# A two-layer gated recurrence and FFN kernel: a new order of all engines, more dummy transposes, h in two buffers

## The reference, cut to what matters

```python
tf    = sigmoid(sum(cond, -1))
decay = exp(-exp(w)) * (0.5 + 0.5 * tf)                 # per batch and channel
ek    = exp(min(F, 30));  ekv = ek * F
nf, df = scan forward of (ekv, ek);  nb, db = scan backward    # a = a * decay + in
euk   = exp(min(u + F, 30))
num   = nf + nb - ekv + euk * F;  den = df + db - ek + euk
y     = sigmoid(x) * num / max(den, 1e-8) * (0.8 + 0.2 * tf)
# layer 0: x += (expert e = argmax(softmax(y @ Wg.T)); prob * 4 * (y @ A[e].T) @ B[e].T)
# layer 1: x += gelu(y @ q(w1).T + b1) @ q(w2).T + b2     # q: sign where |w| >= 0.7 * mean|w|
```

## Time and profile before

| what | value |
|---|---|
| median of 3 runs | 109.0 us (108.44 to 109.6) |
| profiled execution: its time | 109.72 us |
| its span in the profile | 107.9 us |
| TensorE busy | 96.6 us, 90% |
| VectorE busy | 90.7 us, 84% |
| ScalarE busy | 80.4 us, 75% |
| GpSimd busy | 66.3 us, 61% |

### The profile page before, as it was taken

The page is one execution under the profiler, slowest core; times in us unless marked ns, Lnnn a source line. Parts: engine busy times, 40 slices in busy tenths (PEclk is TensorE's granted clock), DMA queues, the critical chain, the costliest instruction groups (busy, mean ns, idle before and its releaser), DMA issues. The chain is left out here.

```text
span 107.9 us, 2103 instructions
## 1 busy us (share of the span) xinstructions
PE 96.6 (90%) x650; PEld 86.6 (80%) x650; DVE 90.7 (84%) x204; ACT 80.4 (75%) x144; POOL 66.3 (61%) x87
## 2 busy tenths in 40 slices
PE   4989958479999989999999998999998897899990
PEld 2759748468789879987988978989998796799980
DVE  3389999959939999999999999799999988968320
ACT  4377998999718689499896599877986699475520
POOL 4179999499920581665998869995755554031220
PEclk9999999965599999999999999999999999999999
DMA  1889999200000000000000000000000001300005
GB/s 61 224 289 319 265 295 399 108 3 0 0 0 0 3 0 6 0 0 0 0 0 3 6 0 0 0 0 0 0 0 6 0 0 54 140 6 3 0 0 194
DMA packets 6886, 6.43 MB, mean 60 GB/s; under 512 B 2370, under 2 KB 6492, under 8 KB 6876
## 3 DMA queue, kind: packets, MB, share of 16 engines
q1 hardware_dynamic: 6868, 6.31, 18.5%
q10 hardware_dynamic: 8, 0.00, 0.0%
HBM read 5.26 MB, written 1.05 MB: 58 GB/s over the span
## 5 line engine op out<-in xcount | busy, mean ns | idle before, releaser
L789 DVE TENSOR_TENSOR_SCAN run<-bank,kv 128x256 f32<-128x256 f32 x32 | 20.3, 671 | 0.2
L300 POOL TENSOR_TENSOR h_lo<-h,h_hi 128x512 fp32r<-128x512 f32 x7 | 9.8, 1409 | 13.3 <-DVE h_hi L308 8.3
L1220 PE MATMUL bank<-xin_hi,w1T 128*128 128x256 f32 x64 | 16.3, 292 | 1.6 <-DVE xin_lo L294 0.9
L1152 PE MATMUL bank<-num,AT 128*128 128x256 f32 x64 | 17.5, 424 | 0.1
L1254 PE MATMUL bank<-w2T,h_hi 128*128 128x256 f32 x64 | 15.9, 285 | 0.3 <-DVE h_lo L300 0.3
L606 ACT ACTIVATE h<-bank,bT 128x256 f32<-128x256 f32 x32 | 13.2, 483 | 3.7 <-DVE h_lo L300 3.0
L1254 PE MATMUL bank<-w2T,h_lo 128*128 128x256 f32 x64 | 15.6, 282 | 0.0
L1220 PE MATMUL bank<-xin_lo,w1T 128*128 128x256 f32 x64 | 15.5, 279 | 0.0
L1152 PEld LDWEIGHTS bank<-num,AT 128*128 128x128 f32 x64 | 13.1, 214 | 2.2 <-issue 0.2
L1168 PE MATMUL bank<-hm,BT 128*128 128x256 f32 x64 | 14.6, 381 | 0.0
L248 POOL TENSOR_TENSOR num<-num,own 128x512 f32<-128x512 f32 x7 | 9.2, 1319 | 8.4 <-DVE num L823 8.4
(11 more groups left out here) (140 smaller groups left out, 232.6 us busy)
## 6 DMA issues: line engine op xcount, KB each, us to landing
w_nat<-in_L_ffn_w_dram SPq DMA_DIRECT2D x2, 1024.0 KB, 8.5
F_nat<-in_fside_BxSxS_dram SPq DMA_DIRECT2D x4, 256.0 KB, 3.5
x_nat<-in_x_dram SPq DMA_DIRECT2D x4, 256.0 KB, 4.9
out_dram<-outb SPq DMA_DIRECT2D x3, 256.0 KB, 2.1
A_nat<-in_L_ffn_A_dram SPq DMA_DIRECT2D x1, 512.0 KB, 5.8
B_nat<-in_L_ffn_Bw_dram SPq DMA_DIRECT2D x2, 256.0 KB, 6.5
out_dram<-outb SPq DMA_DIRECT2D x2, 128.0 KB, 1.9
wv_rows<-in_L_cond_w_dram SPq DMA_DIRECT2D x2, 1.0 KB
```

Of the source, the lines that this page charges most:

```text
L300: eng.tensor_tensor(h_lo[:, b % 2, 2 * j:2 * j + 2], h32[:, 2 * j:2 * j + 2], h_hi[:, b % 2, 2 * j:2 * j + 2].bitcast(F32), ALU.subtract). ...
L789: dve.tensor_tensor_scan(run[:, r, c, q], decay_ps[:, l, c, b:b + 1].broadcast_to([P, T]), kv[:, b, c, q], 0.0, ALU.mult, ALU.add).then_in ...
L1152: mm = pe.matmul(bank[H_BANK + k][:, (m % 2) * T:(m % 2 + 1) * T], AT[:, c, m * P:(m + 1) * P], num_at(0, b)[:, c], start=(c == 0), stop=( ...
L1220: mm = pe.matmul(bank[g_bank[g]][:, (f % 2) * T:(f % 2 + 1) * T], w1T[:, c, f * P:(f + 1) * P], part[:, b % 2, c], start=(c == 0 and part ...
```

## The change

h32 gets a second buffer, chosen by b % 2; the gelu then waits for h_low of b - 2, and h_high waits for h_low of b - 1. For layer 1's gate, the 1 is added to tanh on GpSimd for all four batches, by a function of its own with two scalar operations (multiply by 1, add 1), and `times_tanh` is a plain multiply on either engine. `warm_up(3)` becomes `warm_up(4)`, and of `keep_warm` 8, 18 and 6 become 0, 19 and 27. All four written orders change.

```diff
-        h32 = sb("h32", [P, NF, T])
+        h32 = sb("h32", [P, 2, NF, T])
...
+        def add_one(b):
+
+            nc.gpsimd.wait_ge(tanh_ready, b + 1)
+            nc.gpsimd.tensor_scalar(sig[:, b], sig[:, b], 1.0, 1.0, ALU.mult, ALU.add).then_inc(one_added, 1)
+
         def times_tanh(eng, b):
-
             r, u = ring(1, b)
-            eng.wait_ge(tanh_ready, b + 1)
-            if eng is nc.vector:
-                eng.wait_ge(num_ready[r], u + 1)
-                eng.scalar_tensor_tensor(num_at(1, b), sig[:, b], 1.0, num_at(1, b), ALU.add, ALU.mult).then_inc(nsig_ready[b], 1)
-            else:
-                eng.tensor_scalar(sig[:, b], sig[:, b], 1.0, None, ALU.add).then_inc(one_added[b], 1)
-                eng.wait_ge(one_added[b], 1)
-                eng.wait_ge(num_ready[r], u + 1)
-                eng.tensor_tensor(num_at(1, b), num_at(1, b), sig[:, b], ALU.mult).then_inc(nsig_ready[b], 1)
+            eng.wait_ge(one_added, b + 1)
+            eng.wait_ge(num_ready[r], u + 1)
+            eng.tensor_tensor(num_at(1, b), num_at(1, b), sig[:, b], ALU.mult).then_inc(nsig_ready[b], 1)
...
         def h_high(eng, b, j):
             eng.wait_ge(h32_ready, NF * b + 2 * j + 2)
+            if b:
+                eng.wait_ge(hlo_ready[j], b)
...
             def gelus(b, j):
                 act.wait_ge(g_psum, NJ * b + j + 1)
-                if b:
-                    act.wait_ge(hlo_ready[j], b)
+                if b >= 2:
+                    act.wait_ge(hlo_ready[j], b - 1)
...
             hidden(3, 0)
             hidden(3, 1)
-            ffn_out(2, 0, 0)
-            ffn_out(2, 0, 1)
-            hidden(3, 2)
             ffn_out(2, 1, 0)
             ffn_out(2, 1, 1)
+            hidden(3, 2)
```

More of the change, by code:

```diff
@@ L420, in _ @@
             gains()
-            clip_keys(pool, 1)
+            times_values(pool, 0)
             factors()
-            times_values(pool, 0)
+            seed(pool, 0, 0, DEN)
+            seed(pool, 0, 1, DEN)
+            seed(pool, 0, 0, NUM)
             times_values(pool, 1)
@@ L426, in _ @@
             clip_keys(pool, 2)
-            seed(pool, 0, 0, NUM)
-            seed(pool, 0, 1, DEN)
-            own_values(pool, 0, 1)
-            times_values(pool, 2)
             add_num(pool, 0, 0)
             times_sigmoid(pool, 0)
+            own_values(pool, 0, 1)
             seed(pool, 0, 1, NUM)
@@ L676, in _ @@
             gelus(0, 0)
+            copy_mask(3)
             gelus(0, 1)
-            copy_mask(3)
+            h_high(act, 0, 0)
+            gelus(0, 2)
+            gelus(0, 3)
+            h_high(act, 0, 1)
             tanh(2)
-            gelus(0, 2)
-            h_high(act, 0, 0)
+            h_high(act, 0, 3)
             h_high(act, 0, 2)
-            h_high(act, 0, 1)
-            gelus(0, 3)
-            xin_high(act, 1)
             act.preload_act_table_set("natural_log_exp_and_others")
             log_den(1, 2)
-            h_high(act, 0, 3)
             reciprocal(1, 2)
@@ L703, in _ @@
             reciprocal(1, 3)
+            result(act, 1)
             act.preload_act_table_set("gelu_and_others")
-            gelus(2, 0)
-            result(act, 0)
             gelus(2, 1)
-            result(act, 1)
+            h_high(act, 2, 1)
             gelus(2, 2)
@@ L909, in _ @@
             forward_chunk(0, 0, DEN, 1)
+            clip_keys(dve, 1)
             inverse_gains()
-            seed(dve, 0, 0, DEN)
             forward(0, 1, DEN)
+            forward(0, 0, NUM)
             place_factors()
@@ L953, in _ @@
-            gate(2)
-            backward(0, 3, DEN)
-            own_keys(1, 0)
-            add_den(0, 3)
-            gate_index(2)
+            forward(0, 2, NUM)
+            forward(0, 3, DEN)
+            select_expert(0, 1)
+            gate(1)
+            select_expert(0, 0)
+            add_den(0, 2)
+            backward(0, 2, NUM)
+            gate_index(1)
+            forward(0, 3, NUM)
+            expert_mask(1)
+            own_keys(1, 0)
+            den_times_rec(0, 2)
+            backward(0, 3, DEN)
@@ L958, in _ @@
+            ratio(0, 2)
+            select_expert(1, 1)
+            select_expert(1, 0)
+            add_den(0, 3)
+            forward(1, 0, NUM)
+            gate(2)
+            backward(0, 3, NUM)
+            gate_index(2)
+            forward(1, 0, DEN)
+            den_times_rec(0, 3)
+            expert_mask(2)
             backward(1, 0, NUM)
             backward(1, 0, DEN)
-            den_times_rec(0, 3)
+            ratio(0, 3)
+            select_expert(2, 0)
             add_den(1, 0)
-            expert_mask(2)
@@ L992, in _ @@
-            add_num(dve, 1, 2)
-            h_low(dve, 0, 3)
-            times_tanh(dve, 2)
-            refine_rec(1, 2)
-            seed(dve, 1, 3, DEN)
-            product(1, 2)
-            h_high(dve, 1, 2)
+            select_expert(3, 0)
+            select_expert(3, 1)
+            refine_rec(1, 1)
+            forward(1, 2, DEN)
+            product(1, 1)
+            xin_high(dve, 1)
+            backward(1, 2, DEN)
+            add_den(1, 2)
+            forward(1, 2, NUM)
+            forward(1, 3, DEN)
@@ L999, in _ @@
+            backward(1, 2, NUM)
+            den_times_rec(1, 2)
+            forward(1, 3, NUM)
+            times_tanh(dve, 2)
+            seed(dve, 1, 3, NUM)
+            seed(dve, 1, 3, DEN)
+            refine_rec(1, 2)
+            product(1, 2)
+            h_low(dve, 0, 3)
             h_low(dve, 1, 1)
@@ L1001, in _ @@
             backward(1, 3, DEN)
+            backward(1, 3, NUM)
             add_den(1, 3)
-            backward(1, 3, NUM)
-            h_low(dve, 1, 3)
+            add_num(dve, 1, 3)
+            h_high(dve, 2, 0)
+            times_tanh(dve, 3)
             den_times_rec(1, 3)
-            times_tanh(dve, 3)
             refine_rec(1, 3)
@@ L1343, in _ @@
             ffn_out(1, 2, 1)
-            hidden(2, 2)
+            place_output(2)
             ffn_out(1, 3, 0)
             ffn_out(1, 3, 1)
+            hidden(2, 2)
             hidden(2, 3)
-            place_output(2)
+            ffn_out(2, 0, 0)
+            ffn_out(2, 0, 1)
             place_output(3)
```

241 lines of the change are left out of this document (109 added, 132 removed).

## The result

The changed kernel took 102.95 us (median of 4 runs, 102.38 to 104.0) against 108.72 for the kernel before on the same chip (4 runs, 108.12 to 109.6): a ratio of 0.942, 95% interval 0.935 to 0.950. Two later comparisons on other chips gave 0.940 (0.934 to 0.947) and 0.943 (0.938 to 0.949). The forecast was 105.3 us with a range of 103.9 to 108.0: right in sign, with a gain too small by 2.3 us, and outside its range. The profiled execution took 102.58 us, its span is 100.8.

What follows compares the result with a forecast made beforehand. It took TensorE and VectorE as nearly level bounds. TensorE's -1.0 (start), -1.96 (clock) and 0.7 of idle gave -3.7, span 107.9 to 104.2, or 105.3 us against the median; range 103.9 to 108.0.

Steps and rivals of the forecast that it cites:

- Both are bounds, nearly level ... TensorE is late first: From 31.43 to 93.35 TensorE idles 2.98 us; VectorE is busy 65.81 of 71.18; a gain in one alone is not kept.
- 2.98 us of idle of which the order can take some. I count 0.7 as taken. That gives -3.7 for TensorE: TensorE behind the first mask: 0.7 us of its idle time removed, on top of -2.96 at the mask, gives -3.7.
- The last xin_lo could end at 86.8 without waits: VectorE from the first ratio at 21.6: 64.2 us of work plus 1.0 of small gaps, against 93.29 before.
- I count about 3 (three locks of 1, a stall of 0.5): VectorE's waits up to the last xin_lo, about 3 us on top of 86.8, where 3.8 were allowed.
- Start of the expert products, "-1.0": TensorE's expert products wait for ScalarE's whole BT copy, expected at 23.65: start at 23.85 instead of 24.84.
- Clock, 1.96 us: More dummy transposes keep TensorE at 2.4 GHz through the first expert products: gain 1.96 us, bounds 0 to 1.96 + 0.84.
- First ratio "to about 21.6": VectorE up to the first ratio: -0.44 us from moved own keys and clip_keys(1), from 22.11 to about 21.6 with the seed.
- Tail, -1.0: ffn_out(2, 0) ahead of hidden(3, 0): 88 matmuls instead of 96 follow the last xin_lo, 10.6 us for 11.59.
- A: TensorE's clock falls all the same near the first expert products, costing 1.96 us back: 107.3 us; chance 0.18.
- B: VectorE keeps the pace: waits for GpSimd's num and seeds use 2 us more than counted: 107.2 us; chance 0.14.
- C: GpSimd falls behind between own_values(1, 1) and add_num(1, 2), VectorE's tanh waits: slower, 110.3 if 5 us late; chance 0.05.
- D: No change: first ratio slips from 21.6 to 23 behind GpSimd's clip_keys(2), TensorE loses the clock: 108.7 us; chance 0.08.

Runs made afterwards that it cites:

- before, new dummies: Kernel before with 19, 29 and 10 dummy transposes in place of 8, 18 and 6, nothing else changed: 0.989 of the kernel before.
- before, TensorE +1.78: Kernel before with TensorE's residual products of batch 2 issued three times, 1.78 us more work: 1.002 of the kernel before.
- before, VectorE +2.36: Kernel before with four more scans to a spare buffer on VectorE, 2.36 us more work: 1.028 of the kernel before.
- before, nine steps moved: Kernel before with nine VectorE steps of batch 2 in another order, such as the multiply by tanh ahead of h_lo(0,3): 0.990 of the kernel before.
- early part alone: Kernel before with the new order only up to the first ratio and first expert products, with 19 and 27 dummies: 0.988 of the kernel before.
- early part, nine steps moved: Kernel before with the new order up to the first expert products, plus nine VectorE steps of batch 2 reordered: 0.978 of the kernel before.
- late part alone: Changed kernel with the old order and old dummies up to the first ratio and first expert products: 0.969 of the kernel before.
- changed, old tail: Changed kernel with ffn_out(2, 0) behind hidden(3, 1) again: 0.952 of the kernel before, median 104.8 us.
- changed, TensorE +1.78: Changed kernel with TensorE's residual products of batch 2 issued three times, 1.78 us more work: 0.950 of the kernel before.
- changed, VectorE +2.36: Changed kernel with four more scans to a spare buffer on VectorE, 2.36 us more work: 0.962 of the kernel before.
- section 1: Extra work on TensorE or VectorE alone: 1.002 and 1.028 in the kernel before, 0.950 and 0.962 in the changed kernel, all against the kernel before.
- section 4: Nine VectorE steps of batch 2 reordered: 0.990 in the kernel before, 0.978 in it with the new order up to the first expert products.
- section 6: Changed kernel repeated: 0.940 and 0.943; with four more dummies 0.942; with ScalarE's cast xin_hi(2) ahead of gelus(1, 3) 0.947, all against the kernel before.
- section 3: Changed kernel with the old 8, 18, 6 dummies: 0.947; kernel before with 19, 29, 10: 0.989, both against the kernel before.
- section 5: Changed kernel with add_one in its old form 0.951, on VectorE for batches 2 and 3 0.954, one h buffer 0.950, ffn_out(2, 0) moved back 0.952.
- the run with the slow add_one: Changed kernel with the four GpSimd add_one in the old form, one scalar operation, 1.50 us for 0.62: 0.951 of the kernel before.

## Why the forecast was wrong in size

The table holds the profiled executions: start of the second ratio and of the last xin_lo on VectorE, the time between, the span, and what lies behind the last xin_lo.

| kernel | second ratio | last xin_lo | between | span | behind |
|---|---|---|---|---|---|
| before | 29.30 | 92.60 | 63.3 | 107.9 | 15.3 |
| before, new dummies | 28.85 | 92.03 | 63.2 | 107.3 | 15.3 |
| before, TensorE +1.78 | 29.42 | 92.30 | 62.9 | 107.6 | 15.3 |
| before, VectorE +2.36 | 28.80 | 95.24 | 66.4 | 110.5 | 15.3 |
| before, nine steps moved | 28.54 | 91.69 | 63.2 | 106.9 | 15.2 |
| early part alone | 28.96 | 90.39 | 61.4 | 105.6 | 15.2 |
| early part, nine steps moved | 28.93 | 90.61 | 61.7 | 105.8 | 15.2 |
| late part alone | 28.88 | 88.47 | 59.6 | 102.9 | 14.4 |
| changed | 26.73 | 86.37 | 59.6 | 100.8 | 14.4 |
| changed, old dummies | 27.83 | 87.95 | 60.1 | 102.3 | 14.4 |
| changed, one h buffer | 27.88 | 87.48 | 59.6 | 102.1 | 14.6 |
| changed, old tail | 26.64 | 86.26 | 59.6 | 101.6 | 15.3 |
| changed, TensorE +1.78 | 26.71 | 87.81 | 61.1 | 102.2 | 14.4 |
| changed, VectorE +2.36 | 26.75 | 91.08 | 64.3 | 105.5 | 14.4 |

Whatever is changed ahead of it, the end is the last xin_lo plus 15.2 to 15.3 us with the old tail and plus 14.3 to 14.6 with the new one. The sum of the end from this point holds in all of them; it does not say which engine made the last xin_lo late, as the row with more TensorE work shows.

- **"Both are bounds, nearly level ... TensorE is late first": wrong.** In the kernel before VectorE was the bound (section 1). Of TensorE's 2.98 us of idle time behind 31.43, the waits that the profile names are 2.0 us for VectorE and 0.67 for a gelu of ScalarE.
- **"2.98 us of idle of which the order can take some. I count 0.7 as taken. That gives -3.7 for TensorE": the step that failed.** Nearly all of it went; from 31 to 87 us 0.3 are left. The sum was capped by an engine that did not set the time, and VectorE was only asked whether it allowed -3.7. What set it was VectorE's stretch from the first ratio's end to the last xin_lo's: 71.18 us before, 65.72 now, 5.46 less.
- **The last xin_lo could end at 86.8 without waits: near, in part by luck.** It ended at 87.06, with waits: work was 63.37 us and not 64.2, waits and gaps 2.35 and not 1.0, and the start 0.26 earlier. From there the forecast's own terms lead on: 107.9 - 93.29 = 14.6 behind it, less 1.0 for the tail, gives a span of 100.4; measured 100.8. **"I count about 3 (three locks of 1, a stall of 0.5)": wrong.** The locks were taken as a property of the operands, which stayed, and they hang on who begins first (section 4). None of the three came in any profiled execution of the changed kernel; the lock that did come, in one, is another (section 6). Even with its about 3 us of waits the forecast's own VectorE path gives 103.4 of span, 0.8 below the 104.2 that it took from TensorE.
- **Start of the expert products, "-1.0": measured -1.76.** The absolute sums began at 18.36, not near 19.1, and the second copy of B ended at 22.93, not 23.65.
- **Clock, 1.96 us: right as a term of TensorE** (6.59 us for the stretch to the mask, now 4.42), but what it is worth in time is not settled. TensorE waits for VectorE later, and in section 3 the old dummies cost 0.4 to 0.7 us by the ratio. But six of the sixteen executions of the changed kernel had lost some clock too (0.983), and the profiled one with the old dummies is 1.6 us above the changed kernel's, 0.7 of it the lock. Executions of the kernel before with a mean clock near 0.983 had a median of 108.9 us (34 of them) and near 0.968 one of 110.0 (39); the changed kernel 102.5 near 1.00 (10) and 103.7 at 0.983 (6).
- **First ratio "to about 21.6": measured 21.34.** What followed it, gate ahead of the thresholds, was not in the sum: the wait of 1.05 us for the weight totals went, and with the second ratio 1.79 us were gained, the second largest piece, though 0.75 of it is less work in that stretch, mostly since a pair of scans moved behind the ratio.
- **Tail, -1.0: measured -0.9**, for the reason given. **add_one, 0.61: 0.62**; at 1.50 it costs 1.1 us, so the choice of the end mattered. **h buffer, 0:** open, 0.2 us in the profiled execution and 0.9 by the median (section 5).
- **Rivals.** A, that the clock falls all the same, did not happen in the profiled execution: the 27 dummies took 3.1 us at full clock, and the windows from 22 to 30 us show 1.00. By the rule in the Trainium skill, "TensorE: Matmul & The Clock Gate", "Part 4: PE-mode transpose", it should have; the trace disagrees, here and in the earlier trace rows. B was the right engine with the wrong sign: VectorE kept the pace, and was itself the one made faster. It is what the early part alone shows. C, GpSimd's queue late: it waits for VectorE (5.1 us at num), never the other way in the long stretch. D, a late first ratio: it came earlier, at 21.34.
- **The rule on locks.** VectorE's two-column threshold, one input, SBUF to SBUF, took 1.30 us beside a GpSimd product and 0.17 without. So a scalar operation does stand still, as the Trainium skill has it ("SBUF — State Buffer", "Who interferes with whom"); the trace agrees. xin_high(1) and clip_keys(1), which the forecast priced at 1.0 us in all by that rule, took 0.43 each and paid nothing; neither began inside a long GpSimd instruction. A cast that did is in the run with the slow add_one: h_hi at 84.21 began inside it and took 0.69, where it takes 0.41 in the changed kernel. The same rows show that not every meeting locks: an add with both inputs in SBUF, inside the same add_one, took its usual 0.69. Why stays open.

```profile
83.14 1.48 POOL L259 TENSOR_SCALAR sig<-sig 128x512 f32<-128x512 f32 x1
```

```profile
83.60 0.69 DVE L248 TENSOR_TENSOR num<-num,own 128x512 f32<-128x512 f32 x1
84.21 0.69 DVE L306 CAST h_hi<-h 128x512 fp32r<-128x512 f32 x1
```

## What to carry to other kernels

An engine with 5% of waits and one with 7.5% are not "level": put a microsecond or two of dead work on each in turn, and two runs tell more than any sum of busy time. They settled the kernel before; in the changed kernel both engines answered, and then neither is the bound alone. Then follow the engine that answered through its own milestones, and forecast its end: its work, its waits, its locks, and the fixed tail behind it; the other engine's idle time is an effect. Where VectorE and GpSimd both read SBUF, place VectorE's PSUM operations beside GpSimd's long ones, and expect that a small operation can lose as much as a large one.
